# VectorE turns o of the first four blocks in phase 2, in 32 by 32 squares out of PSUM

## The chip, the cores and the metric

The kernel runs on one core of a Trainium2 chip. The metric is the device time in microseconds (us) of one execution; the median of three runs of the kernel before is 740.78 us (740.58 to 740.94).

## What is computed

`adj` is a 4096 x 4096 matrix, `x` is 4096 x 128, all in fp32. Two graph layers follow each other, each with a residual sum and a layer norm:

```python
scale = sum(d_list * filt * d_list, axis=0)
o = adj @ (scale[:, None] * (adj @ (x @ W0)))          # layer 0: z = adj @ x, v = scale * (z @ W0), o = adj @ v
x1 = layernorm(x + o + bias)
inn = (adj   / rowsum(adj))   @ x1 @ W_in              # layer 1: y
outt = (adj.T / rowsum(adj.T)) @ x1 @ W_out            # layer 1: z2
result = layernorm(x1 + inn + outt)
```

## The kernel before

`adj` is cut into 8 x 8 chunks of 512 x 512 (1 MB each). A chunk is loaded by SyncE into one of six ring slots (`raw`), ScalarE rounds it to `hi` (four activations of 128 x 512 where row sums are taken as well), and VectorE computes `lo = raw - hi` (`low(n)`, one instruction over 128 x 2048 in the phases of interest). A product of a chunk with a block of x or v is then 12 matmuls on TensorE (`product`): four of hi by the vector's high part, four of hi by its low part, four of lo by its high part (lines 647, 652, 657). The slot is free for the next load when TensorE has released the chunk. Each engine's instructions stand in an order written out by hand, all of it by the chunk number n; engines meet at counting semaphores only.

The result of a product lies in PSUM as features x rows (128 x 512 per block of 512 rows). The row-wise work needs rows x features, so the accumulator has to be turned.

Phase 1 (chunks below N1) computes z, v and the first part of o. Phase 2 (N1 to N2, 38 chunks) finishes o, block by block from I = 7 down to 0, and takes the first part of y from the same chunks: a chunk (J, I) with J > I is used for o and, behind it, for y (`y_product`). Blocks 7 to 4 have 7 - I chunks in phase 2, since their other part of o was saved in phase 1; blocks 3 to 0 (I < LEAD = 4) have 8 chunks each. The phase after N2 reads the other copy of adj for z2 and then the rest of y; it needs every x1 block in the order 7 to 0.

When o of block I is complete in `accB[:, I % 2]`, the following happens in phase 2, the numbers being chunk numbers after the block's last one, `last2[I]`:

- VectorE, after `low(last2 + 2)`: `o_sum(I)`. For blocks 3 to 0 this is one copy of 128 x 512 from PSUM to `turned` in SBUF (line 501).
- TensorE, after the products of `last2 + 2`: `turn_o(I)`, four transposes by the identity matrix of 128 x 128 each, from `turned` to the PSUM buffer `nat` (line 687). For block 0 this stands before the very last y product of the phase.
- VectorE, after `low(last2 + 4)`: `x1_block(I)` adds `nat` to the rows in SBUF (line 526) and takes the moments (lines 508, 511); ScalarE takes the square root in its turn (line 366) and can round no further chunk before it; then `x1_parts(I)` scales the rows and splits them into x_hi and x_lo (lines 535 to 539).

Only after that come `low(last2 + 5)` and the next ones. The chunk numbers of block 0 run over into the next phase: its `o_sum` stands behind `low(N2 + 1)`, its `x1_block` behind `low(N2 + 3)`.

Of the kernel before, what the change touches and what calls it, by code (L numbers as in the profile page):

```python
# [8 lines left out]
ALU = mybir.AluOpType  # L9
# [3 lines left out]
P = 128  # L13
TPB = 4
# [5 lines left out]
LEAD = 4  # L20


def graph_kernel(nc, x_t, adj_b, adjT_b, coef_t, W0, bias, W_in, W_out, ident_d, out):
# [10 lines left out]
    NB = adj_b.shape[0]  # L34
# [39 lines left out]
    w_out_at = {last_z2[J] + (3 + J - HB if J >= HB else 2): J for J in range(NB)}  # L74
    w_in_at = {last4[I] + 3: I for I in range(NB - 1)}
    assert not set(w_out_at) & set(w_in_at)
    NAT_H, NAT_Y = {}, {}
    for k, n in enumerate(sorted(list(w_out_at) + list(w_in_at))):
        if n in w_out_at:
            NAT_H[w_out_at[n]] = 2 * NB + k  # L80
        else:
            NAT_Y[w_in_at[n]] = 2 * NB + k
    NAT_Y[NB - 1] = 4 * NB - 1


    both = [n for n in range(N1, N2) if chunks[n][0] > chunks[n][1]]
    y_behind, y_rest = {}, list(both)
    for n in range(N1 + 3, N2):
        y_behind[n] = [m for m in y_rest if m <= n - (2 if n >= N1 + 6 else 3)]
        y_rest = y_rest[len(y_behind[n]):]  # L90
# [47 lines left out]
    def with_sums(n):  # L138

        J, I = chunks[n]  # L140
        return J <= I and I >= LEAD if n < N1 else n < N2 or is_z2[n]
# [4 lines left out]
    for n in range(N4):  # L146
        hi_at.append([hi_count + (t if n < LEAD * NB or with_sums(n) else 0) + 1 for t in range(TPB)])
        lo_at.append([lo_count + t * parts[n] // TPB + 1 for t in range(TPB)])
        hi_count, lo_count = hi_at[n][-1], lo_at[n][-1]


    NAT_O = NB

    def o_saved(I):

        return 2 * NB - 1 - LEAD - I

    with ExitStack() as ctx:
        def sb(name, shape, dt=F32):
            return ctx.enter_context(nc.sbuf_tensor(name, shape, dt))  # L160

        def pb(name, banks):
            return ctx.enter_context(nc.psum_tensor(name, [P, banks, BLK], F32))

        def sem(name):
            return ctx.enter_context(nc.semaphore(name))
# [16 lines left out]
        rows = sb("rows", [P, NT, P])  # L183
        part = sb("part", [P, NB - 1, BLK])
        turned = sb("turned", [P, 2, BLK])
# [21 lines left out]
        accB = pb("accB", 2)  # L207
        nat = pb("nat", 2)
# [28 lines left out]
        s_os = sem("o_taken")  # L237
        s_ty = sem("turned_y_ready")
        s_nat = sem("nat_read")
        s_x1 = sem("x1_ready")  # L240
# [7 lines left out]
        s_o = sem("o_done")  # L248
        s_n = sem("nat_filled")
# [9 lines left out]
        def block_of(I):  # L259
            return slice(TPB * I, TPB * I + TPB)  # L260
# [52 lines left out]
        def _(act):  # L313
# [38 lines left out]

            def turn_h(J):
                act.wait_ge(s_rel, rank[last_z2[J]])
                act.wait_ge(s_n, NAT_H[J] - 1)
                nc.scalar.activation(turned[:, NAT_H[J] % 2], z2_acc[J % HB], ACT.Copy).then_inc(s_tz, 1)

# [79 lines left out]
        def _(dve):  # L437
# [53 lines left out]

            def o_sum(I):
                u = 2 * NB - 1 - I
                dve.wait_ge(s_n, u - 1)
                if I == NB - 1:
                    dve.wait_ge(s_v, NB)
                    dve.wait_ge(s_rel, rank[N1 - 1])
                else:
                    dve.wait_ge(s_o, NB - 1 - I)
                if I < LEAD or I == NB - 1:  # L500
                    nc.vector.tensor_copy(turned[:, u % 2], accB[:, I % 2]).then_inc(s_os, 1)
                    return
                dve.wait_ge(s_os, o_saved(I) - 1)
                nc.vector.tensor_tensor(turned[:, u % 2], accB[:, I % 2], part[:, I], ALU.add).then_inc(s_os, 1)

            def moments(k, I, tiles):
                for t in tiles:
                    last = nc.vector.bn_stats(stats[:, t], rows[:, TPB * I + t])
                then(last)
                for t in tiles:  # L510
                    last = nc.vector.bn_aggr(mv[:, k % 2, t], stats[:, t])
                last.then_inc(s_var, 1)
# [9 lines left out]

            def x1_block(I):
                k = NB - 1 - I
                dve.wait_ge(s_n, NAT_O + k + 1)
                nc.vector.tensor_tensor(rows[:, block_of(I)], nat[:, k % 2].rearrange("p (t f) -> p t f", t=TPB),
                                        rows[:, block_of(I)], ALU.add).then_inc(s_nat, 1)
                dve.wait_ge(s_nat, k + 1)
                moments(k, I, range(TPB))

            def x1_parts(I):
# [23 lines left out]
            def update(r, t, bank):  # L555

                row = TPB * r + t
                return nc.vector.scalar_tensor_tensor(rows[:, row], bank[:, P * t:P * t + P], deg[:, 1, row:row + 1],  # L558
                                                      rows[:, row], ALU.mult, ALU.add)
# [63 lines left out]
            k = NB + r  # L623
            dve.wait_ge(s_out, k - NB - 1)
            for t in range(TPB):
                dve.wait_ge(s_n, NAT_Y[r] + t + 1)
                last = update(r, t, last_bank[t])
# [3 lines left out]
            for t in range(TPB):  # L631
                row = TPB * r + t
                last = nc.vector.tensor_scalar(rows[:, row], rows[:, row], mv[:, k % 2, t, 0:1],
                                               rstd[:, k % 2, t:t + 1], ALU.subtract, ALU.mult)
# [4 lines left out]
        def _(pe):  # L639
            def product(acc, r_hi, r_lo, K, n, first, last):  # L640

                h, l = hi[slot_of[n]], lo[slot_of[n]]

                def by_hi(t):
                    if t == 0 or hi_at[n][t] > hi_at[n][t - 1]:
                        pe.wait_ge(s_hi, hi_at[n][t])
                    nc.tensor.matmul(acc, r_hi[:, TPB * K + t], h[:, t], start=(first and t == 0), stop=False)  # L647
                    if n == 0 and t == 0:
                        pe.wait_ge(s_x0, 2)
                    elif n in x_from and t == 0:  # L650
                        pe.wait_ge(s_xlo, K)
                    nc.tensor.matmul(acc, r_lo[:, TPB * K + t], h[:, t], start=False, stop=False)  # L652

                def by_lo(t):
                    if t == 0 or lo_at[n][t] > lo_at[n][t - 1]:
                        pe.wait_ge(s_lo, lo_at[n][t])
                    return nc.tensor.matmul(acc, r_hi[:, TPB * K + t], l[:, t], start=False,  # L657
                                            stop=(last and t == TPB - 1))

                early = n == 0  # L660
                for t in range(TPB):
                    by_hi(t)
                    if early and t:
                        by_lo(t - 1)
                for t in range(TPB - 1 if early else 0, TPB):
                    mm = by_lo(t)
                return mm
# [15 lines left out]
            def transposes(e):  # L683
                room(e)
                for t in range(TPB):
                    to = slice(P * t, P * t + P)
                    mm = nc.tensor.transpose(nat[:, e % 2, to], turned[:, e % 2, to], ident[:])  # L687
                mm.then_inc(s_n, 1)
# [7 lines left out]
            def turn_o(I):  # L696
                pe.wait_ge(s_os, o_saved(I))
                if I == NB - 1:
                    pe.wait_ge(s_small, 16 * len(small))
                transposes(NAT_O + NB - 1 - I)  # L700
# [14 lines left out]
            def y_product(n):  # L715
                J, I = chunks[n]
                pe.wait_ge(s_x1, NB - J)
                if J == NB - 1:
                    pe.wait_ge(s_tz, NB)
                    if I <= NB - 4:  # L720
                        pe.wait_ge(s_ys, NB - 3 - I)
                product(accA[:, I % 2], x_hi, x_lo, J, n, J == NB - 1, J == I + 1).then_inc(s_rel, 1)
# [5 lines left out]
            for n in range(N1):  # L728
                J, I = chunks[n]
# [25 lines left out]
            for n in range(N1, N2):  # L755
                J, I = chunks[n]
                if n == first2[I]:
                    pe.wait_ge(s_os, o_saved(I + 2))
                mm = o_product(n, n == first2[I], n == last2[I])
                if n == last2[I]:  # L760
                    mm.then_inc(s_o, 1)
                elif J <= I:
                    mm.then_inc(s_rel, 1)
                if n == N1:
                    turn_o(NB - 1)
                for m in y_behind.get(n, []):
                    y_product(m)
                if n == N1 + 3:
                    turn_o(NB - 2)
                for I in range(NB - 3, 0, -1):  # L770
                    if n == last2[I] + (3 if I == NB - 3 else 2):
                        turn_o(I)
            for m in y_rest[:-1]:
                y_product(m)
            turn_o(0)
            y_product(y_rest[-1])

            for n in range(N2, N4):
                if is_z2[n]:
                    I, J = chunks[n]  # L780
# [7 lines left out]
                else:  # L788
                    J, I = chunks[n]
# [5 lines left out]
                if n in w_out_at:  # L795
                    J = w_out_at[n]
                    pe.wait_ge(s_tz, NB + J + 1)
                    by_rows(NAT_H[J], w_out)
                if n in w_in_at:
                    I = w_in_at[n]  # L800
# [3 lines left out]
            for t in range(TPB):  # L804
                to = slice(P * t, P * t + P)
# [34 lines left out]
```

## Time and profile before

| | value |
|---|---|
| median of three runs | 740.78 us |
| the profiled execution | 740.59 us |
| its span, first to last instruction | 738.8 us |
| TensorE busy | 728.8 us, 99% |
| VectorE busy | 564.1 us, 76% |
| ScalarE busy | 511.2 us, 69% |
| mean granted TensorE clock | 0.998 |

The profiled execution's own time is 1.8 us above its span. Times in the rows count from the start of the span. Phase 2 lies at about 261 to 442 us. A group in the rows is named by the line of the kernel; a row of the timeline gives the start, the length, and in brackets how long the engine had been idle and who ended that. Where a row says x4, the length is that of the four together, which overlap.

### The profile page before, as it was taken

What the parts mean: (1) busy time and instruction counts of PE and PEld (TensorE: products, weight loads), DVE (VectorE), ACT (ScalarE), POOL (GpSimd) and SP (SyncE); (2) the same over time, 40 slices, a digit from 0 to 9 for tenths busy, and PEclk for the clock granted to TensorE, in tenths of its full rate; (3) what the DMA queues carried; (4) which work ended last, traced back from release to release, by engine and by line L of the source; (5) the groups of instructions that cost most, each with busy time, mean ns of one, the idle gap of its engine ahead of it and who ended that gap; (6) DMA issues with size and microseconds to landing.
All of it is one profiled execution on the core that took longest, in us unless ns stands there. A gap on an engine that the chain in (4) does not pass through costs nothing.

```text
span 738.8 us, 9134 instructions
## 1 busy us (share of the span) xinstructions
PE 728.8 (99%) x3312; PEld 602.9 (82%) x3312; DVE 564.1 (76%) x663; ACT 511.2 (69%) x1304; POOL 18.5 (3%) x15
## 2 busy tenths in 40 slices
PE   8999999999999999999999999999999999999996
PEld 5888888888888888888888888888888888888885
DVE  5998987563735478867583748997898999999996
ACT  5888985734625454657474547998999888876862
POOL 1122200000000000000000000000000000000000
PEclk9999999999999999999999999999999999999999
DMA  8999995555545346776657459999999999999991
GB/s 345 424 426 421 427 412 185 200 215 212 201 160 199 138 159 241 265 273 244 228 171 254 151 217 374 386 385 386 365 335 389 385 365 383 383 354 351 348 360 34
DMA packets 35532, 217.02 MB, mean 294 GB/s; under 512 B 3616, under 2 KB 8480, under 8 KB 9760
## 3 DMA queue, kind: packets, MB, share of 16 engines
q1 hardware_dynamic: 35072, 215.79, 76.4%
q10 hardware_dynamic: 416, 0.66, 0.3%
q8 instruction: 26, 0.43, 0.2%
q14 instruction: 18, 0.15, 0.1%
HBM read 214.34 MB, written 2.10 MB: 293 GB/s over the span
## 4 chain that ended last, share of the span: by engine, by line
PE 96%; DMA 2%; DVE 1%; SPq 0%; ACT 0%; issue 0%; DVEq 0%
PE accA L647 14%; PE accA L652 14%; PE accA L657 14%; PE accB L647 12%; PE accB L652 12%; PE accB L657 12%; PE accC L657 6%; PE accC L647 6%; PE accC L652 6%; PE nat L680 3%; DMA raw<-in_adjT_b 2%; PE nat L687 0%; DVE lo L451 0%; SPq L280 0%; DVE rows L558 0%; ACT hi L329 0%
## 5 line engine op out<-in xcount | busy, mean ns | idle before, releaser
L451 DVE TENSOR_TENSOR lo<-raw,hi 128x2048 fp32r<-128x2048 f32 (+2 forms) x236 | 463.7, 1988 | 114.7 <-ACT hi L323 101.7
L323 ACT ACTIVATE hi<-raw 128x512 fp32r<-128x512 f32 x512 | 315.5, 622 | 70.2 <-DMA raw<-in_adjT_b 44.6
L647 PE MATMUL accA<-hi,x_hi 128*128 128x512 f32 x448 | 175.7, 392 | 1.9 <-ACT hi L329 1.9
L652 PE MATMUL accA<-hi,x_lo 128*128 128x512 f32 x448 | 174.4, 389 | 0.0
L657 PE MATMUL accA<-lo,x_hi 128*128 128x512 f32 x448 | 120.4, 389 | 0.1
L647 PE MATMUL accB<-hi,v_hi 128*128 128x512 f32 x256 | 100.4, 392 | 0.0
L647 PEld LDWEIGHTS accA<-hi,x_hi 128*128 128x128 f32 x448 | 84.2, 188 | 19.7 <-issue 2.4
L652 PE MATMUL accB<-hi,v_lo 128*128 128x512 f32 x256 | 99.7, 389 | 0.0
L657 PEld LDWEIGHTS accA<-lo,x_hi 128*128 128x128 f32 x448 | 84.0, 188 | 18.0 <-DVE lo L451 0.6
L652 PEld LDWEIGHTS accA<-hi,x_lo 128*128 128x128 f32 x448 | 84.1, 188 | 16.8
L323 ACT ACTIVATION_READ_ACCUMULATOR hi<-raw 128x1 f32 x512 | 97.3, 190 | 0.0
L331 ACT ACTIVATE hi<-raw 128x2048 fp32r<-128x2048 f32 x42 | 80.1, 1914 | 24.7 <-DMA raw<-in_adjT_b 24.7
L329 ACT ACTIVATE hi<-raw 128x512 fp32r<-128x512 f32 x128 | 70.3, 621 | 15.2 <-DMA raw<-in_adjT_b 15.1
L647 PE MATMUL accC<-hi,x_hi 128*128 128x512 f32 x192 | 75.0, 390 | 0.0
L652 PE MATMUL accC<-hi,x_lo 128*128 128x512 f32 x192 | 74.7, 389 | 0.0
L657 PE MATMUL accB<-lo,v_hi 128*128 128x512 f32 x256 | 68.5, 389 | 0.0
L657 PEld LDWEIGHTS accB<-lo,v_hi 128*128 128x128 f32 x256 | 48.1, 188 | 10.1
L647 PEld LDWEIGHTS accB<-hi,v_hi 128*128 128x128 f32 x256 | 48.1, 188 | 9.8
L652 PEld LDWEIGHTS accB<-hi,v_lo 128*128 128x128 f32 x256 | 48.1, 188 | 9.8
L657 PE MATMUL accC<-lo,x_hi 128*128 128x512 f32 x192 | 51.6, 390 | 0.1
L647 PE MATMUL accB<-hi,x_hi 128*128 128x512 f32 x128 | 50.3, 393 | 0.0
L652 PE MATMUL accB<-hi,x_lo 128*128 128x512 f32 x128 | 49.8, 389 | 0.0
(74 smaller groups left out, 454.7 us busy)
## 6 DMA issues: line engine op xcount, KB each, us to landing
raw<-in_adjT_b SPq DMA_DIRECT2D x137, 1024.0 KB, 4.9
raw<-in_adj_b SPq DMA_DIRECT2D x64, 1024.0 KB, 5.2
rows<-in_x_t SPq DMA_DIRECT2D x8, 256.0 KB, 10.7
out<-rows SPq DMA_DIRECT2D x7, 256.0 KB, 5.8
raw<-in_adjT_b ACTq DMA_DIRECT2D x1, 512.0 KB, 5.4
raw<-in_adjT_b SPq DMA_DIRECT2D x1, 512.0 KB, 6.7
out<-rows SPq DMA_DIRECT2D x1, 128.0 KB, 1.8
out<-rows ACTq DMA_DIRECT2D x1, 128.0 KB, 1.8
```

Of the source, the lines that this page charges most:

```text
L323: nc.scalar.activation(hi[slot][:, t], raw[slot][:, t], ACT.Copy, accum_out=to[:, TPB * K + t, C:C + 1]).then_inc(s_hi, 1)
L329: nc.scalar.activation(hi[slot][:, t], raw[slot][:, t], ACT.Copy).then_inc(s_hi, 1)
L331: nc.scalar.activation(hi[slot][:], raw[slot][:], ACT.Copy).then_inc(s_hi, 1)
L451: nc.vector.tensor_tensor(lo[slot][:, at], raw[slot][:, at], hi[slot][:, at], ALU.subtract).then_inc(s_lo, 1)
L647: nc.tensor.matmul(acc, r_hi[:, TPB * K + t], h[:, t], start=(first and t == 0), stop=False)
L652: nc.tensor.matmul(acc, r_lo[:, TPB * K + t], h[:, t], start=False, stop=False)
L657: return nc.tensor.matmul(acc, r_hi[:, TPB * K + t], l[:, t], start=False, stop=(last and t == TPB - 1))
L680: mm = nc.tensor.matmul(nat[:, e % 2, to], turned[:, e % 2, to], w[:], start=True, stop=True)
```

## The change

For blocks 3 to 0, `o_sum` no longer copies: VectorE reads `accB` in squares of 32 partitions by 32 columns and writes each square transposed to its place in `turned`. One instruction takes the four tiles of a block at once (32 x 4 x 32), so there are 16 instructions per block, in the place where the copy stood. `x1_block` of these blocks adds `turned` instead of `nat` and waits for nothing of TensorE. TensorE's `turn_o` of blocks 3 to 0 goes, and the numbers of the uses of `nat` behind it move down by four. ScalarE's first two copies to `turned` in the next phase get a wait for the last x1 block in addition, since VectorE now reads `turned` there.

```diff
             def o_sum(I):
                 u = 2 * NB - 1 - I
-                dve.wait_ge(s_n, u - 1)
+                if I >= LEAD - 2:
+                    dve.wait_ge(s_n, u - 1)
                 if I == NB - 1:
                     dve.wait_ge(s_v, NB)
                     dve.wait_ge(s_rel, rank[N1 - 1])
-                else:
-                    dve.wait_ge(s_o, NB - 1 - I)
-                if I < LEAD or I == NB - 1:
                     nc.vector.tensor_copy(turned[:, u % 2], accB[:, I % 2]).then_inc(s_os, 1)
+                    return
+                dve.wait_ge(s_o, NB - 1 - I)
+                if I < LEAD:
+                    of = accB[:, I % 2].rearrange("p (t n) -> p t n", t=TPB)
+                    to = turned[:, u % 2].rearrange("p (t f) -> p t f", t=TPB)
+                    for a in range(0, P, 32):
+                        for b in range(0, P, 32):
+                            last = nc.vector.transpose(to[b:b + 32, :, a:a + 32], of[a:a + 32, :, b:b + 32])
+                    last.then_inc(s_os, 1)
                     return
...
             def x1_block(I):
                 k = NB - 1 - I
-                dve.wait_ge(s_n, NAT_O + k + 1)
-                nc.vector.tensor_tensor(rows[:, block_of(I)], nat[:, k % 2].rearrange("p (t f) -> p t f", t=TPB),
-                                        rows[:, block_of(I)], ALU.add).then_inc(s_nat, 1)
-                dve.wait_ge(s_nat, k + 1)
+                if I < LEAD:
+                    dve.wait_ge(s_os, o_saved(I))
+                    then(nc.vector.tensor_tensor(rows[:, block_of(I)], rows[:, block_of(I)],
+                                                 turned[:, (NB + k) % 2].rearrange("p (t f) -> p t f", t=TPB), ALU.add))
...
             def turn_h(J):
                 act.wait_ge(s_rel, rank[last_z2[J]])
+                if NAT_H[J] < 2 * NB - LEAD + 2:
+                    act.wait_ge(s_x1, NB)
...
-                for I in range(NB - 3, 0, -1):
+                for I in range(NB - 3, LEAD - 1, -1):
                     if n == last2[I] + (3 if I == NB - 3 else 2):
                         turn_o(I)
-            for m in y_rest[:-1]:
+            for m in y_rest:
                 y_product(m)
-            turn_o(0)
-            y_product(y_rest[-1])
```

On TensorE the end of phase 2 read before as follows; `accA<-lo5` is the last but one y product, `accA<-hi2` the last, and `nat<-ident` the turn of block 0:

```order
1643 L652 MATMUL accA<-hi5_66,x_lo 128x512
1644 L657 MATMUL accA<-lo5_65,x_hi 128x512 [waits lo_ready]
1645 L657 MATMUL accA<-lo5_65,x_hi 128x512 x3
1646 L687 MATMUL nat<-ident,turned 128x128 [waits nat_read,o_taken]
1647 L687 MATMUL nat<-ident,turned 128x128 x3
1648 L647 MATMUL accA<-hi2_57,x_hi 128x512 [waits hi_ready,x1_ready]
```

The same place with the change:

```order
1637 L668 MATMUL accA<-hi5_66,x_lo 128x512
1638 L673 MATMUL accA<-lo5_65,x_hi 128x512 [waits lo_ready]
1639 L673 MATMUL accA<-lo5_65,x_hi 128x512 x3
1640 L663 MATMUL accA<-hi2_57,x_hi 128x512 [waits hi_ready,x1_ready]
1641 L668 MATMUL accA<-hi2_57,x_lo 128x512
```

The four transposes are gone, and nothing stands in their place. Likewise at the turns of blocks 3, 2 and 1.

On VectorE, block 0 at the start of the next phase, before; `lo3`, `lo0`, `lo1` are the subtractions of chunks N2 + 1, N2 + 2 and N2 + 3:

```order
247 L451 TENSOR_TENSOR lo3_59<-raw3_58,hi3_60 128x2048 [waits hi_ready,dve_step]
248 L501 COPY turned<-accB 128x512 [waits o_done,nat_filled]
249 L451 TENSOR_TENSOR lo0_50<-raw0_49,hi0_51 128x2048 [waits hi_ready]
250 L451 TENSOR_TENSOR lo1_53<-raw1_52,hi1_54 128x2048 [waits hi_ready]
251 L526 TENSOR_TENSOR rows<-nat,rows 128x512 [waits nat_filled]
252 L508 BN_STATS stats<-rows 128x6 [waits nat_read]
```

And with the change:

```order
250 L454 TENSOR_TENSOR lo3_59<-raw3_58,hi3_60 128x2048 [waits hi_ready,dve_step]
251 L511 STREAM_TRANSPOSE turned<-accB 32x4x32 [waits o_done]
252 L511 STREAM_TRANSPOSE turned<-accB 32x4x32 x15
253 L454 TENSOR_TENSOR lo0_50<-raw0_49,hi0_51 128x2048 [waits hi_ready]
254 L454 TENSOR_TENSOR lo1_53<-raw1_52,hi1_54 128x2048 [waits hi_ready]
255 L538 TENSOR_TENSOR rows<-rows,turned 128x512 [waits o_taken]
256 L519 BN_STATS stats<-rows 128x6 [waits dve_step]
```

Sixteen instructions stand where one did, ahead of two subtractions for which TensorE will ask, and the sum that follows them no longer waits for TensorE.

## Rows read from the trace of the kernel before

**Rows 1.** Page, parts 1 and 2: busy time by engine, and TensorE's clock in 40 slices

```profile
PE 728.8 (99%) x3312; PEld 602.9 (82%) x3312; DVE 564.1 (76%) x663; ACT 511.2 (69%) x1304; POOL 18.5 (3%) x15
...
PEclk9999999999999999999999999999999999999999
```

**Rows 2.** Waits of TensorE over the whole span: total, times, longest

```profile
PE accA L647 <- ACT hi L329: 1.9, 1, 1.9
PE accB L726 <- DVE warm L577: 1.2, 1, 1.2
PE accB L807 <- ACT turned L412: 0.4, 1, 0.4
```

**Rows 3.** The chain that ended last, around blocks 3, 2, 1, 0: start, length, what

```profile
333.59 0.91 PE accA L657 x4
334.50 0.44 PE nat L687 x4
336.79 0.92 PE accB L657 x4
...
369.44 0.91 PE accA L657 x4
372.63 0.91 PE accB L657 x4
...
405.27 0.91 PE accB L657 x4
407.99 0.91 PE accA L657 x4
...
411.19 0.92 PE accB L657 x4
...
441.13 0.91 PE accA L657 x4
...
444.32 0.91 PE accA L657 x4
```

**Rows 4.** Groups by line on VectorE: shapes, count, busy, mean ns of one

```profile
L508 DVE BATCH_NORM_STATS2 stats<-rows 128x6 f32<-128x128 f32 x64 | 14.0, 281 | 0.5
L558 DVE SCALAR_TENSOR_TENSOR rows<-nat,deg,rows 128x128 f32<-128x128 f32 x28 | 7.8, 342 | 0.0
L501 DVE COPY turned<-accB 128x512 f32<-128x512 f32 x5 | 3.4, 688 | 2.5 <-PE accB L657 2.5
```

**Rows 5.** Timeline of VectorE around block 0: start, length, instruction, idle before

```profile
438.15 0.69 DVE L501 COPY turned<-accB 128x512 f32<-128x512 f32 x1
443.68 2.29 DVE L451 TENSOR_TENSOR lo<-raw,hi 128x2048 fp32r<-128x2048 f32 x1 [4.84 <-ACT hi L323]
446.67 2.29 DVE L451 TENSOR_TENSOR lo<-raw,hi 128x2048 fp32r<-128x2048 f32 x1 [0.70 <-ACT hi L323]
448.88 0.69 DVE L526 TENSOR_TENSOR rows<-nat,rows 128x512 f32<-128x512 f32 x1
...
454.29 4.65 DVE L451 TENSOR_TENSOR lo<-raw,hi 128x2048 fp32r<-128x2048 f32 x2
```

**Rows 6.** Timeline of TensorE's weight loads for the lo matmuls of chunk N2 + 4

```profile
457.53 0.87 PEld L657 LDWEIGHTS accC<-lo,x_hi 128*128 128x128 f32 x4
```

**Rows 7.** Timeline of VectorE around block 3

```profile
323.72 0.69 DVE L501 COPY turned<-accB 128x512 f32<-128x512 f32 x1 [1.30 <-PE accB L657]
...
334.97 0.69 DVE L526 TENSOR_TENSOR rows<-nat,rows 128x512 f32<-128x512 f32 x1 [4.27 <-PE nat L687]
...
340.38 4.65 DVE L451 TENSOR_TENSOR lo<-raw,hi 128x2048 fp32r<-128x2048 f32 x2
```

**Rows 8.** Timeline of VectorE around blocks 2 and 1

```profile
356.85 0.69 DVE L501 COPY turned<-accB 128x512 f32<-128x512 f32 x1 [1.20 <-PE accB L657]
...
366.83 2.29 DVE L451 TENSOR_TENSOR lo<-raw,hi 128x2048 fp32r<-128x2048 f32 x1 [5.43 <-ACT hi L323]
...
396.76 0.68 DVE L501 COPY turned<-accB 128x512 f32<-128x512 f32 x1
...
405.34 2.29 DVE L451 TENSOR_TENSOR lo<-raw,hi 128x2048 fp32r<-128x2048 f32 x1 [3.06 <-ACT hi L323]
409.38 0.69 DVE L526 TENSOR_TENSOR rows<-nat,rows 128x512 f32<-128x512 f32 x1 [1.74 <-PE nat L687]
```

**Rows 9.** Stretch of 442.5 to 520 us: busy by engine, clock, DMA share

```profile
442.50:520.00 77.50, 77.50 (x343) 64.14 (x343) 65.81 (x46) 68.14 (x219) 0.00 (x0) 1.00 0.98 383
```

More of the change, by code:

```diff
@@ L79, in graph_kernel @@
         if n in w_out_at:
-            NAT_H[w_out_at[n]] = 2 * NB + k
+            NAT_H[w_out_at[n]] = 2 * NB - LEAD + k
         else:
-            NAT_Y[w_in_at[n]] = 2 * NB + k
-    NAT_Y[NB - 1] = 4 * NB - 1
+            NAT_Y[w_in_at[n]] = 2 * NB - LEAD + k
+    NAT_Y[NB - 1] = 4 * NB - LEAD - 1
     both = [n for n in range(N1, N2) if chunks[n][0] > chunks[n][1]]
@@ L524, in x1_block @@
                 k = NB - 1 - I
-                dve.wait_ge(s_n, NAT_O + k + 1)
-                nc.vector.tensor_tensor(rows[:, block_of(I)], nat[:, k % 2].rearrange("p (t f) -> p t f", t=TPB),
-                                        rows[:, block_of(I)], ALU.add).then_inc(s_nat, 1)
-                dve.wait_ge(s_nat, k + 1)
+                if I < LEAD:
+                    dve.wait_ge(s_os, o_saved(I))
+                    then(nc.vector.tensor_tensor(rows[:, block_of(I)], rows[:, block_of(I)],
+                                                 turned[:, (NB + k) % 2].rearrange("p (t f) -> p t f", t=TPB), ALU.add))
+                else:
+                    dve.wait_ge(s_n, NAT_O + k + 1)
+                    nc.vector.tensor_tensor(rows[:, block_of(I)], nat[:, k % 2].rearrange("p (t f) -> p t f", t=TPB),
+                                            rows[:, block_of(I)], ALU.add).then_inc(s_nat, 1)
+                    dve.wait_ge(s_nat, k + 1)
                 moments(k, I, range(TPB))
```

## The prediction

> **What bounds the kernel now.** Read the page's engine shares first: TensorE is busy 728.8 us of a span of 738.8, at the full granted clock in every slice (2.4 GHz, of the two levels) [rows 1]. Then its waits: in the whole span it waited three times, 3.5 us together, and none of the three is in phase 2 or the phase behind it (they are the first product, the warm-up and the last four matmuls) [rows 2]. So from the second product to the last one TensorE runs without a hole, and the chain that ended last is TensorE's own row of matmuls [rows 3]. Two things follow. Whatever leaves TensorE's queue shortens the kernel by the time it took there; and whatever happens on VectorE costs nothing until a subtraction (`lo`) is finished later than TensorE asks for it. VectorE has 24% of idle time as a mean, but the mean doesn't decide; what does is the slack at the four places where work is added.
>
> **TensorE: four turns go.** I read their price from the pace of the products. Without a turn the lo matmuls of two successive products start 2.72 us apart (405.27 to 407.99). With a turn between them the distance is 3.20 (333.59 to 336.79), 3.19 (369.44 to 372.63), 3.20 (407.99 to 411.19) and 3.19 (441.13 to 444.32) [rows 3]. The excess is 0.48 + 0.47 + 0.48 + 0.47 = 1.90 us. The transposes themselves are only 0.44 of each in the chain; the few hundredths left are slightly wider steps of the first matmuls behind them, which go too. No wait is in that excess (TensorE had none), so all of it comes back: -1.90 us. The wait for `o_taken` that stood before each turn goes at no gain.
>
> **VectorE: 16 transposes for one copy, four times.** The trace shows no such instruction. Call T the time of the 16. Each handles 128 elements per partition out of PSUM. Lower bound: the nearest small instructions in a row, each starting before the last has ended. The mean step is 14.0 us / 64 = 0.22 for the statistics over 128 elements (SBUF) and 7.8 / 28 = 0.28 for the PSUM operand; T is 3.5 to 4.5 us. If instead each starts when the last has ended, the durations count: 16 x 0.342 = 5.5 us. Upper bound: each takes as long as the copy of the whole bank, 16 x 0.688 = 11.0 us, as if the square cost four times the pace of a copy [rows 4]. Between ends this far apart I take 5.5, from the row that is nearest (a PSUM operand, 128 elements, full duration), because successive transposes write other partitions than the one before and I see no row in which that overlaps.
>
> The Trainium skill bears on just that: "VectorE: DVE Perf Modes", section "Two Vector instructions with no wait between them", says that an instruction whose output starts in another group of 32 partitions than the last output waits until all earlier ones have finished. By it all 16 are held, and T is the 5.5 rather than the 4.5; no run here has shown it yet.
>
> **What hides T.** Block 0 is the tight place. The copy starts at 438.15; the next subtraction starts at 443.68 because ScalarE isn't done with its chunk before [rows 5]. So T may be 443.68 - 438.15 = 5.53 us and nothing moves at all. There are 0.70 us of idle time before the next subtraction (446.67), so up to 6.23 the sum at 448.88 starts where it did. From there VectorE runs through the moments and the parts and reaches the subtraction of N2 + 4 at 454.29; one takes 2.29, so it ends at 456.58 [rows 5]. TensorE loads the weights of its lo matmuls at 457.53 [rows 6]: slack 0.95. With block 0's turn gone TensorE comes 0.47 earlier against VectorE (the three earlier turns shift both alike, since VectorE's place here is set by ScalarE, the loads and TensorE's releases), which leaves 0.48. Hence TensorE waits if T is above 6.23 + 0.48 = 6.71 us, that is 0.42 us per transpose. With T = 5.5 it waits for nothing.
>
> Block 3: the transposes start at 323.72. The two subtractions behind them need 4.65 and may then start when VectorE pleases; before, the sum waited until 334.97 for TensorE's turn, 4.27 us of it idle [rows 7]. Now it needs T + 4.65 from 323.72, so up to T = 334.97 - 323.72 - 4.65 = 6.6 the sum is not later than it was. The subtraction behind x1_parts starts at 340.38 and ends at 342.67 [rows 7]; it is that of last2 + 5, whose lo matmuls stand three products behind the one at 336.79 (last2 + 3, last2 + 4, a y product, last2 + 5), at 336.79 + 3 x 2.72 = 344.95. Their weights are loaded 0.4 us ahead, and the turn's 0.48 goes: 344.95 - 0.4 - 0.48 = 344.07, a slack of 1.4. So block 3 bears T up to 6.6 + 1.4 = 8.0. Blocks 2 and 1: from the copy to the second subtraction behind it are 366.83 - 356.85 = 9.98 and 405.34 - 396.76 = 8.58 us, of which the first subtraction needs 2.29; so T is free up to 7.7 and 6.3 us, and the idle 1.74 us that the sum of block 1 waited for the turn is more reserve [rows 8]. None of these is as tight as block 0.
>
> **The rest, at nothing.** The sum in `x1_block` reads SBUF rather than PSUM at the same 128 x 512 elements; it is one instruction behind cover in each block. ScalarE's first new wait stands behind its chunk N2 + 31, some 26 chunks of 2.72 us behind the x1 block for which it waits, so it costs nothing. The renumbering of `nat` moves no instruction. Loads are asked for by TensorE's releases; in the stretch behind phase 2 the DMA engines are at 0.98 and 383 GB/s [rows 9], but that is TensorE's own pace (1.05 MB per 2.72 us is 386 GB/s), and since every load is asked for 1.90 us earlier, it lands earlier as well.
>
> The sum against the profiled execution: 740.59 - 1.90 = 738.69 us, span 738.8 - 1.9 = 736.9. The profiled execution lies 0.19 below the median of the runs shown, so the median should be 740.78 - 1.90 = 738.88 us, 0.26% less. What a measurement of this kernel can tell from no change is about 0.2%, or 1.48 us.
>
> **Rival A, a part is given back at block 0.** T lies between 7.1 and 9: then TensorE waits at chunk N2 + 4 for T - 6.71 (and at block 3 for T - 8.0 above that). At T = 8 the time is 740.78 - 1.90 + 1.3 = 740.2; at T = 9 with both waits, it is 740.78 - 1.90 + 2.3 + 1.0 = 742.2. All of this case is "no difference". For it: fp32 squares of 32 at half the pace of a copy would add 0.13 us each to 0.342, T = 7.6. Against it: every other VectorE instruction in the rows runs fp32 out of PSUM at the pace of its elements (512 in 0.688 us, 128 in 0.342) [rows 4].
>
> **Rival B, slower.** The place is the same, the lo of N2 + 4, and block 3 joins. The price: at T = 11.0 TensorE waits 11.0 - 6.71 = 4.3 us behind block 0 and 11.0 - 8.0 = 3.0 behind block 3, 740.78 - 1.90 + 7.3 = 746.2. The kernel gets slower from T of about 9.05 (0.57 us per transpose) on, where the two waits together exceed 1.90 + 1.48. Against it: it wants a transpose that costs nearly as much as a whole bank's copy, on a quarter of the elements. In the skill, "VectorE: DVE Perf Modes", section "The three transpose paths", has VectorE at 311 ns for 128 x 128 in bf16, in squares of 32; by that figure, an estimate, T would be about 5.0. The same page's rules send a 128 x 128 transpose to TensorE; the rows say the reverse is paid for here, because the time is taken from the engine that has no idle time and given to one that has.
>
> **Rival C, the turns give nothing.** If the excess of 0.48 around a turn were a wait of TensorE's queue that another wait would replace, such as the next chunk's `hi`, the time would stay 740.8. The waits of TensorE speak against it: none is listed there [rows 2].
>
> **How the numbers follow.** Forecast (T below 6.7, or a wait of less than 0.42): 0.77, of which a little is lost to the bound lying only 0.4 us from the gain. Rival A 0.13, rival B 0.06, rival C 0.04. So faster by over 0.2% is 0.75; within 0.2% 0.18; slower 0.07. The likeliest time is 738.9. The range takes the forecast with the scatter of the runs (0.2 us either side), and rival A's lower half: 738.4 to 740.2.
>
> **What would show it.** Products at 2.72 us across all four former turns; 16 transposes at 0.34 us or less per step; no wait of TensorE for `lo` between 440 and 470 us; the sum of block 3 earlier than 334.97, and that of block 1 about 1.7 us earlier; the next subtraction of block 0 still waiting for ScalarE, if briefly. Wrong would be: a step above 0.42 us, and with it a wait of TensorE for the `lo` of N2 + 4 about 16 us behind the end of block 0's o.

## The result, and the profile after

Twelve runs of the kernel after have a median of 739.02 us (738.70 to 739.28), twelve of the kernel before 740.82 us. The ratio is 0.9974 with a 95% interval of 0.9966 to 0.9981: 1.80 us less, where 1.90 were forecast. The profiled execution took 738.70 us with a span of 736.9 us; before it was 740.59 and 738.8, so 1.89 less in one and 1.9 in the other.

The page of the kernel after, parts 1 and 2, answers to [rows 1]:

```profile
PE 727.3 (99%) x3296; PEld 601.5 (82%) x3296; DVE 581.2 (79%) x723; ACT 511.7 (69%) x1304; POOL 18.6 (3%) x15
...
PEclk9999999999999999999999999999999999999998
```

TensorE has 16 instructions fewer, VectorE is busy 17.1 us longer, and the time still fell. The waits of TensorE after are the same three as in [rows 2], with nothing in phase 2:

```profile
PE accA L663 <- ACT hi L330: 1.7, 1, 1.7
PE accB L742 <- DVE warm L593: 1.2, 1, 1.2
PE accB L821 <- ACT turned L415: 0.4, 1, 0.4
```

The chain that ended last, after, at the places of the four former turns (start, length, what), answers to [rows 3]:

```profile
333.60 0.91 PE accA L673 x4
336.32 0.91 PE accB L673 x4
...
368.96 0.91 PE accA L673 x4
371.68 0.91 PE accB L673 x4
...
407.04 0.91 PE accA L673 x4
409.76 0.91 PE accB L673 x4
...
439.68 0.91 PE accA L673 x4
442.40 0.91 PE accA L673 x4
```

All four distances are 2.72 us now. The first pair starts where it did (333.60 against 333.59); the lo matmuls of the last product of phase 2 start at 442.40 against 444.32, 1.92 us earlier. From there to the end of the span it is 294.5 us in both, so nothing is added or lost behind it.

VectorE after: all transposes, and its timeline around block 3, which answers to [rows 7]:

```profile
L511 DVE STREAM_TRANSPOSE turned<-accB x64: 303/312/323, 323.7 to 441.7; 32x128 f32<-32x128 f32 x64
```

```profile
323.73 5.20 DVE L511 STREAM_TRANSPOSE turned<-accB 32x128 f32<-32x128 f32 x16 [1.31 <-PE accB L673]
328.97 4.49 DVE L454 TENSOR_TENSOR lo<-raw,hi 128x2048 fp32r<-128x2048 f32 x2
333.38 0.69 DVE L538 TENSOR_TENSOR rows<-rows,turned 128x512 f32<-128x512 f32 x1
...
338.77 4.65 DVE L454 TENSOR_TENSOR lo<-raw,hi 128x2048 fp32r<-128x2048 f32 x2
```

T, the time of the 16, is 5.20 us: one transpose takes 0.312 us, and the next starts 0.325 after it. The two subtractions follow without a pause, and the sum starts at 333.38, which is 1.6 us earlier than before, although VectorE had 4.5 us more to do: before, it had stood still 4.27 us for TensorE's turn and 1.7 us for ScalarE.

Block 0 after, which answers to [rows 5], and the weight loads that answer to [rows 6]:

```profile
436.79 5.21 DVE L511 STREAM_TRANSPOSE turned<-accB 32x128 f32<-32x128 f32 x16
442.03 2.29 DVE L454 TENSOR_TENSOR lo<-raw,hi 128x2048 fp32r<-128x2048 f32 x1
445.36 2.29 DVE L454 TENSOR_TENSOR lo<-raw,hi 128x2048 fp32r<-128x2048 f32 x1 [1.04 <-ACT hi L324]
447.57 0.68 DVE L538 TENSOR_TENSOR rows<-rows,turned 128x512 f32<-128x512 f32 x1
...
452.96 4.66 DVE L454 TENSOR_TENSOR lo<-raw,hi 128x2048 fp32r<-128x2048 f32 x2
```

```profile
455.61 0.87 PEld L673 LDWEIGHTS accC<-lo,x_hi 128*128 128x128 f32 x4
```

The lo of N2 + 4 is the first of the two subtractions in the row at 452.96. It ends at 452.96 + 2.29 = 455.25 and is wanted at 455.61. The reserve was 0.95 us and is 0.36; 0.48 was forecast. Of T, 1.04 us more fit before the sum moves, and 0.36 more before TensorE waits: the bound is 6.6 us (forecast 6.71).

### The profile page after: what moved, and what is told of

The parts are those of the page before. It is cut to its first block, busy times and chain, and to the rows that moved or that the text cites. A ratio compares the mean times of both kernels' runs of the same rounds, so it can differ in the third digit from the quotient of the medians.

```text
span 736.9 us, 9156 instructions
## 1 busy us (share of the span) xinstructions
PE 727.3 (99%) x3296; PEld 601.5 (82%) x3296; DVE 581.2 (79%) x723; ACT 511.7 (69%) x1304; POOL 18.6 (3%) x15
## 4 chain that ended last, share of the span: by engine, by line
PE 96%; DMA 2%; DVE 1%; SPq 0%; ACT 0%; issue 0%; DVEq 0%
PE accA L663 14%; PE accA L668 14%; PE accA L673 14%; PE accB L663 12%; PE accB L668 12%; PE accB L673 12%; PE accC L673 6%; PE accC L668 6%; PE accC L663 6%; PE nat L696 3%; DMA raw<-in_adjT_b 2%; DVE lo L454 0%; PE nat L703 0%; SPq L281 0%; DVE rows L574 0%; ACT hi L330 0%
```

## Experiments

**1. The four turns put back as dead work.**

```diff
+            def dead_turn(I):
+                pe.wait_ge(s_nat, NB - LEAD)
+                for t in range(TPB):
+                    to = slice(P * t, P * t + P)
+                    nc.tensor.transpose(nat[:, (NB - 1 - I) % 2, to], ident[:], ident[:])
...
+                for I in range(LEAD - 1, 0, -1):
+                    if n == last2[I] + 2:
+                        dead_turn(I)
-            for m in y_rest:
+            for m in y_rest[:-1]:
                 y_product(m)
+            dead_turn(0)
+            y_product(y_rest[-1])
```

> The kernel after, with TensorE's four turns of blocks 3 to 0 put back in their old places as dead work: four transposes of the identity matrix each into the free buffer nat, which nobody reads and nobody waits for. VectorE still does the real turning. Theory Q (what the change gained is the time of the four turns in TensorE's queue, and VectorE's part is free): 739.0 + 1.9 = 740.9 us, and the distance between lo matmuls across a turn is 3.20 again. Rival W (the gain is in the waits: x1_block no longer waits for TensorE, so ScalarE and VectorE run ahead): stays at 739.0 to 739.3.

Measured: 741.04 us, ratio to before 1.0001 (0.9992 to 1.0010); the kernel before took 740.98 us on the same chip. The chain shows the old distance again, 337.16 - 333.96 = 3.20:

```profile
333.96 0.91 PE accA L673 x4
334.87 0.44 PE nat L722 x4
337.16 0.92 PE accB L673 x4
```

Here x1_block waits for no turn, VectorE and ScalarE have the work and the order of the kernel after, and the whole gain is gone. So it is TensorE's time, and the removed waits of the others were worth nothing that can be measured. Theory Q stands, W falls.

**2. A copy instead of the 16 transposes.**

```diff
-                    for a in range(0, P, 32):
-                        for b in range(0, P, 32):
-                            last = nc.vector.transpose(to[b:b + 32, :, a:a + 32], of[a:a + 32, :, b:b + 32])
+                    last = nc.vector.tensor_copy(to, of)
```

> The kernel after, with one copy of 128 x 512 in place of the 16 transposes (so o of blocks 3 to 0 is added unturned; the result is not the reference's there). VectorE has 4 x 4.5 = 18 us less to do. Theory Q: the transposes are hidden entirely, so 739.0 (738.9 to 739.1). Rival: VectorE's added work costs something by its load on SBUF and PSUM or by small delays: 738.5 or less.

Measured: 739.09 us, ratio 0.9974 (0.9965 to 0.9984), as the kernel after. The eighteen microseconds (4 x 4.5) by which the transposes take longer than a copy cost nothing. Its timeline around block 0 also shows how much room there is without them:

```profile
437.05 0.68 DVE L509 COPY turned<-accB 128x512 f32<-128x512 f32 x1
440.14 2.29 DVE L454 TENSOR_TENSOR lo<-raw,hi 128x2048 fp32r<-128x2048 f32 x1 [2.41 <-ACT hi L324]
445.61 2.29 DVE L454 TENSOR_TENSOR lo<-raw,hi 128x2048 fp32r<-128x2048 f32 x1 [3.17 <-ACT hi L324]
```

The first subtraction starts 440.14 - 437.05 = 3.1 us behind the copy, not 5.53 as in [rows 5]. There ScalarE's rounding of that chunk started 2.9 us behind the start of the copy, since it waited for the load; in all thirteen other traces it starts 0.3 to 0.7 us behind the start of the copy or of the transposes. Only one trace of the kernel before is kept, so it is not shown whether the late load belongs to that execution or to that kernel. The second stands 8.56 us behind the copy's start (8.52 in [rows 5]), and less 2.29 for the first that is a bound of 6.3 us for T, as forecast.

**3. Sixteen more transposes at block 0.**

```diff
+                    squares = [(a, b) for a in range(0, P, 32) for b in range(0, P, 32)]
+                    spare = part[:, I].rearrange("p (t f) -> p t f", t=TPB)
+                    for a, b in squares[:16] if I == 0 else []:
+                        nc.vector.transpose(spare[b:b + 32, :, a:a + 32], of[a:a + 32, :, b:b + 32])
...
```

> The kernel after, with 16 more transposes of accB ahead of block 0's own, into a part of SBUF that nobody reads before it is overwritten. T of block 0 goes from 5.2 to 10.4 us. Theory S (what VectorE may take is the slack at chunk N2 + 4, up to T = 6.25 without a shift and 6.61 without a wait, from the trace after; forecast 6.71): TensorE waits 10.4 - 6.6 = 3.8 us once for the lo of N2 + 4: 742.8 us. Rival M (VectorE is busy 79% on the mean, so 5.2 us more are absorbed): 739.0.

Measured: 742.90, 744.35, 742.76 and 744.40 us, ratio 1.0035 (1.0021 to 1.0049). The profiled one is of 742.90. Its waits of TensorE, those that are new:

```profile
PE accC L676 <- DVE lo L454: 2.2, 1, 2.2
...
PE accC L666 <- ACT hi L324: 0.7, 1, 0.7
```

It is chunk N2 + 4, as forecast; ScalarE is late as well there, since its square root waits for VectorE's moments (454.21 us) and the rounding of N2 + 4 stands behind it. The chain in this trace:

```profile
457.65 2.21 DVE lo L454
459.86 0.04 issue
459.91 1.20 PE accC L676 x4
462.93 0.91 PE accC L676 x4
```

Against the kernel after, the next lo matmuls (those of N2 + 5) start 462.93 - 458.72 = 4.2 us later. This execution's TensorE was 0.41 us behind already before the wait (by the timelines its lo matmuls of N2 + 3 start at 453.53 against 453.12). That leaves 3.8 for a forecast of 3.8; the two executions of 742.8 us lie 3.8 us above the median of the kernel after as well.

The two waits make 2.9 us of the 3.8. The rest is in wider steps. The hi matmuls of the chunk follow ScalarE's activations of 0.61 us each (pairs start at 455.26, 455.80, 456.39 and 457.01, where 0.45 apart is usual), and the first matmuls behind the long wait are slower too. The timeline of TensorE has there:

```profile
459.91 1.20 PE L676 MATMUL accC<-lo,x_hi 128*128 128x512 f32 x4 [2.16 <-DVE lo L454]
...
462.76 1.07 PE L676 MATMUL accC<-lo,x_hi 128*128 128x512 f32 x4
```

That is 2.85 us from lo matmuls to lo matmuls, where 2.72 is usual. M falls: a mean idle share of VectorE of 21% absorbs nothing beyond the 6.6 us at this place. The second group of times is taken up in experiment 9.

**4. Sixteen more at block 3 instead** (the same edit with `I == 3`).

> The same 16 more transposes at block 3 instead of block 0, T = 10.4 us there. Theory S with that block's own slack (forecast bound 8.0; from the trace after the lo of last2 + 5 ends at 341.06 and its weights are loaded at 344.1, so 5.2 + 3.0 = 8.2): TensorE waits 2.2 us for that lo: 741.2 us. If the bound of a block were the same everywhere, 742.8 as at block 0; by rival M 739.0.

Measured: 741.23 us, ratio 1.0003 (0.9994 to 1.0013): 2.2 us more than the kernel after, as theory S had it, from the block's own reserve (10.4 - 2.2 = 8.2). The wait is again for the lo behind x1_parts:

```profile
PE accB L676 <- DVE lo L454: 1.6, 2, 1.4
```

**5. Eight more at block 0** (the edit against experiment 3).

```diff
-                    for a, b in squares[:16] if I == 0 else []:
+                    for a, b in squares[:8] if I == 0 else []:
```

> The kernel after with 8 more transposes at block 0 (half of the earlier padding), T = 24 x 0.325 = 7.8 us. Theory S: TensorE waits for all of what T has above 6.6 us and for nothing below it: 7.8 - 6.6 = 1.2 us, 739.0 + 1.2 = 740.2 us, with one wait, for the lo of N2 + 4. If instead the price were proportional to the added work (16 more cost 3.8 to 4.6 us), 8 more would cost 1.9 to 2.3 us: 740.9 to 741.3.

Measured: 739.76 us, ratio 0.9987 (0.9978 to 0.9996), so 0.7 us above the median of the kernel after, which was not measured beside it. On the same chip as this run the kernel of experiment 6, whose block 0 is that of the kernel after, took 738.64 us, which makes it 1.1. The profiled chain has the lo matmuls of N2 + 5 at 459.74 against 458.72, 1.0 us later. All three are nearer to 1.2 than to 1.9 or more. Together with experiment 3 the price is a line with a threshold, not a proportion: T of 5.2, 7.8 and 10.4 costs 0, 1.0 and 3.8 us in the traces. From 7.8 to 10.4 the price rises by 2.8 for 2.6 us of T, about one for one.

**6. The squares in another order.**

```diff
+                    squares = [(a, b) for a in range(0, P, 32) for b in range(0, P, 32)]
+                    if I == 3:
+                        squares = [(a, b) for b in range(0, P, 32) for a in range(0, P, 32)]
+                    if I == 1:
+                        squares = [(a, (a + k) % P) for k in range(0, P, 32) for a in range(0, P, 32)]
+                    tiles = [slice(0, 2), slice(2, 4)] if I == 2 else [slice(0, 4)]
+                    for a, b in squares:
+                        for t in tiles:
+                            last = nc.vector.transpose(to[b:b + 32, t, a:a + 32], of[a:a + 32, t, b:b + 32])
```

> The kernel after with the squares in another order: block 3 with the column of squares outside (the output stays in one group of 32 partitions for four instructions, the input changes), block 1 along diagonals (both change each time), block 2 with each square cut in two instructions of two tiles, the same input and output partitions twice; block 0 as it was. Theory H (an instruction starts only when the last has ended if either its input or its output starts in another group of 32 partitions than before): blocks 3 and 1 keep T = 5.2 us; in block 2 the second of each pair (0.245 us long) starts before the first has ended, as the statistics do (a step some 0.08 shorter than the duration), so T = 16 x (0.26 + 0.16) = 6.7 us. Rival (transposes never overlap): block 2 takes 32 x 0.26 = 8.3 us. Rival (the output alone decides): block 3 takes 12 x 0.24 + 4 x 0.325 = 4.2 us. The time stays at 739.0 in all cases but the 8.3 us, which would cost some tenths.

Measured: 738.64 us, ratio 0.9973 (0.9962 to 0.9984). Blocks 3, 2 and 1 in its timeline:

```profile
323.70 5.21 DVE L517 STREAM_TRANSPOSE turned<-accB 32x128 f32<-32x128 f32 x16 [1.34 <-PE accB L679]
...
356.34 6.33 DVE L517 STREAM_TRANSPOSE turned<-accB 32x64 f32<-32x64 f32 x32 [1.27 <-PE accB L679]
...
395.81 5.21 DVE L517 STREAM_TRANSPOSE turned<-accB 32x128 f32<-32x128 f32 x16
```

Three orders, one T of 5.21: it is enough that either side changes its partitions. In block 2 three single instructions, one behind the other, are:

```profile
356.51 0.20 DVE L517 STREAM_TRANSPOSE turned<-accB 32x64 f32<-32x64 f32 x1
356.72 0.24 DVE L517 STREAM_TRANSPOSE turned<-accB 32x64 f32<-32x64 f32 x1
356.90 0.20 DVE L517 STREAM_TRANSPOSE turned<-accB 32x64 f32<-32x64 f32 x1
```

From the first of a pair (356.72, 0.24 long) to the second, on the same partitions, it is 0.18, so they overlap. From the second of the pair before (356.51, 0.20 long) to the next pair it is 0.21: that one waits for the end. Theory H holds, and both rivals fall: 6.33 us for block 2 is far from 8.3, and 5.21 for block 3 from 4.2. The 0.4 us by which 6.33 is under the forecast of 6.7 come from the steps: the held one is 0.21 where 0.26 was taken, the overlapping one 0.18 where it was 0.16.

**7. VectorE turns block 4 too, in the old place** (the limits of the change go from 4 to 5 blocks, with this sum ahead of the transposes).

```diff
-                if I < LEAD:
+                if I < TURN:
+                    if I >= LEAD:
+                        dve.wait_ge(s_os, o_saved(I) - 1)
+                        then(nc.vector.tensor_tensor(accB[:, I % 2], accB[:, I % 2], part[:, I], ALU.add))
```

> VectorE turns block 4 too (sum with the saved part in place in PSUM, then 16 transposes), in the old place behind low(last2 + 2); TensorE's turn of block 4 goes. TensorE's queue gives back 0.48 us. But VectorE has no idle time there: it goes from x1 of block 5 straight on. In the trace after, its sum of block 4 starts at 295.4; with 5.9 us of sum and transposes the lo of last2 + 3 ends at 303.6 and is wanted at 302.8, and x1_block comes 4 us later, so the lo of last2 + 5 ends at 313.5 and is wanted at 311.8. Theory S: -0.48 + 1.7 = +1.2, 740.2 us. Rival Q alone (each turn taken off TensorE gains its 0.48): 738.5.

Measured: 740.70 us, ratio 1.0000 (0.9991 to 1.0009). The turn taken away is more than given back. The loss is 1.7 us against the median of the kernel after, not measured beside it, and 2.1 us against the kernel of experiment 6 (738.64) on the same chip. In the traces it is 1.95: the lo matmuls of the last product of phase 2 start at 444.50 against 442.40 in the chains, and 0.15 of that this execution was behind already ahead of block 4. The direction was right, the size of 1.2 was 0.8 too small, by a slip in my sum: the two late subtractions cost 0.8 and then, on top of it, 1.7; I had counted only the second, and 2.5 - 0.48 is 2.0. TensorE's wait in the trace, and VectorE's timeline there:

```profile
PE accB L676 <- DVE lo L455: 1.8, 2, 1.3
```

```profile
295.54 0.69 DVE L509 TENSOR_TENSOR accB<-accB,part 128x512 f32<-128x512 f32 x1
296.27 5.20 DVE L514 STREAM_TRANSPOSE turned<-accB 32x128 f32<-32x128 f32 x16
301.50 4.49 DVE L455 TENSOR_TENSOR lo<-raw,hi 128x2048 fp32r<-128x2048 f32 x2
...
311.31 4.66 DVE L455 TENSOR_TENSOR lo<-raw,hi 128x2048 fp32r<-128x2048 f32 x2
```

**8. The same, at a place with room.**

```diff
-                    if n == last2[I] + (3 if I == NB - 3 else 2):
+                    if n == last2[I] + (3 if I == NB - 3 else 4 if I == 4 else 2):
                         o_sum(I)
-                    if n == last2[I] + 4:
+                    if n == last2[I] + (6 if I == 4 else 4):
                         x1_block(I)
```

(and ScalarE's square root for it moves by two chunks as well)

> As the one before it, but block 4's sum and transposes stand behind low(last2 + 4), and its x1_block, x1_parts and ScalarE's square root behind chunk last2 + 6, where the lo are ahead of TensorE. Theory S: every lo is in time (tightest last2 + 7, 0.9 us of slack), so the whole 0.48 us comes: 738.5 us. If block 4's x1 or the lo are late by more than I work out, 739 to 740.

Measured: 738.47 us, ratio 0.9968 (0.9956 to 0.9981). TensorE waits nowhere in phase 2. In the timeline of TensorE the lo matmuls on either side of the former turn of block 4 start at 300.42 and 303.14, 2.72 us apart; in the kernel after they start at 300.32 and 303.52, 3.20 apart. Between different chips 0.5 us isn't told apart, so this kernel and the kernel after ran again on one chip:

> The kernel after once more, on the same chip and beside the next one. 738.9 to 739.0; its distance to the next one is what is asked.

> The kernel in which VectorE turns block 4 too, behind low(last2 + 4), once more. Theory Q: 0.48 us less than the kernel after on this chip, with spans that differ by the same once the times of the first product are taken off. If it is level with it, the fifth turn is paid for elsewhere.

Measured: 739.02 us (ratio 0.9975, 0.9965 to 0.9985) and 738.54 us (ratio 0.9970, 0.9958 to 0.9981). The difference of the medians is 0.48 us, the price of one turn. The intervals of the two ratios overlap, but five of the six executions (738.36 to 738.55) lie below all nine of the kernel after (738.72 to 739.23); the sixth, at 739.44, is the profiled one, and experiment 9 says where it lost its time. So theory Q holds for the fifth turn too, by the gap in the timelines and by these executions together. This version is the fastest measured. With experiment 7 it shows that the same 5.9 us of VectorE's work cost 2.0 us net or gain 0.5, by where they stand.

**9. The two groups of times.** The kernel of experiment 3 twice more.

> The kernel with 16 more transposes at block 0 once more, for its trace: its runs fell into two groups, about 742.8 us (two) and 744.4 us (two). Theory S gives 742.8 and has no second group. Theory C: TensorE's idle time of some 3 us at chunk N2 + 4 lets its granted clock fall for a while in some executions; then a trace at 744.4 shows slices behind 460 us at a lower clock or products above 2.72 us apart. Theory L: a load or ScalarE comes late as well, then there is a second wait.

> The same kernel a third time, for the same question: 742.8 us with products 2.72 us apart behind the wait, or 744.4 us with a place that shows where 1.6 us more go (theory C: a lower granted clock; theory L: a second wait).

Measured: 744.28 and 742.67 us, one of each group. The stretches of 455 to 460 and 460 to 465 us (busy by engine, granted clock, DMA), in the execution of 744.28:

```profile
455.00:460.00 5.00, 2.83 (x9) 1.51 (x10) 4.87 (x8) 5.00 (x17) 0.00 (x0) 0.96 0.68 274
460.00:465.00 5.00, 5.00 (x17) 3.91 (x16) 4.68 (x3) 5.00 (x19) 0.00 (x0) 0.70 0.45 152
```

and in the one of 742.67:

```profile
455.00:460.00 5.00, 2.81 (x9) 1.49 (x10) 4.82 (x9) 5.00 (x16) 0.00 (x0) 1.00 0.67 277
460.00:465.00 5.00, 5.00 (x23) 4.13 (x22) 4.67 (x3) 5.00 (x18) 0.00 (x0) 1.00 0.59 210
```

The waits of TensorE before it are the same 2.2 us for lo in both. In one the granted clock then is 0.70 as a mean of five microseconds, that is 1.2 GHz for a good part of them, and TensorE gets through 17 matmuls instead of 23. Its timeline has single matmuls start 0.43 us apart there (461.37, 461.79, 462.22), where 0.23 is usual, until 463.04. In its chain it is from the lo matmuls after the wait to the next ones 464.14 - 459.52 = 4.62 us instead of 3.02:

```profile
459.52 2.05 PE accC L676 x4
464.14 0.92 PE accC L676 x4
466.88 0.91 PE accB L676 x4
```

1.6 us, the distance of the two groups. Theory C holds; L falls, since there is no wait in one that isn't in the other. The low clock is seen in this one trace. The other two executions of the slower group (744.35 and 744.40 us) have no trace; their mean clock of 0.996 and 0.994, against 0.998 in all three of the faster group, says the same of them. Why the clock fell in three of six executions with the same waits is open.

It is not only the added work that brings it. The profiled execution of 739.44 us in experiment 8 waited 2.2 us for the hi of its first product, and its stretches of 5 to 10 and 10 to 15 us read:

```profile
5.00:10.00 5.00, 2.79 (x10) 1.45 (x9) 2.05 (x4) 1.60 (x4) 0.00 (x0) 0.90 1.02 404
10.00:15.00 5.00, 5.00 (x18) 3.95 (x18) 4.38 (x6) 4.43 (x10) 0.00 (x0) 0.76 1.02 424
```

The clock is 0.90 and 0.76, and the execution is 0.9 us above the median of its kernel. In the trace of experiment 3 the same wait was 2.4 us, and the clock stayed at 1.00. Single executions of other kernels that lie 0.6 to 1.0 us above their median have a mean clock of 0.995 or 0.996 too, one of the kernel before among them (741.79 us, 0.995); where they lost it isn't on record.

## Why the prediction was right

- **TensorE, -1.90 us.** Right: the excess of a turn between two products was 3.20 - 2.72, all of it came back (442.40 against 444.32, -1.92), and experiment 1 takes it away again by putting only the turns back. Rival C, that the excess hid a wait, has nothing left.
- **T.** Taken at 5.5 from the row of the nearest duration, 5.20 measured. The time doesn't test it: any T below 6.6 gives the same, and the copy of 0.7 us in experiment 2 did; it is the trace that does. The lower bound of 3.5 to 4.5, from instructions that overlap, was wrong because these don't: the trace after has steps of 0.325 with durations of 0.312. By what the Trainium skill states ("VectorE: DVE Perf Modes", section "Two Vector instructions with no wait between them") they shouldn't, and experiment 6 agrees: changing the partitions on the input side alone, on the output side alone or on both gives the same T, and a pair that keeps both overlaps.
- **The cover.** Right in size: the bound at block 0 was 6.71, the trace after gives 6.6, experiments 3 and 5 find the wait at the named chunk and its price at 3.8 and 1.0 us. One step on the way was wrong: I took the 5.5 us from the copy to the next subtraction as the rule. That was a late load in the one trace of the kernel before; experiment 2 has 3.1, and in the kernel after the subtraction followed the transposes without the pause that I had named as a sign. The sum still held because the reserve that decides lies one subtraction further. Block 3's bound of 8.0 is confirmed within 0.2 by experiment 4 (2.2 us for T = 10.4).
- **What hides where.** Block 3's sum came 1.6 us earlier. Block 1's started at 406.70 against 409.38 in [rows 8], 2.68 earlier, of which 0.95 is the gain of the two turns before it: 1.7, as forecast. Its row after is

```profile
406.70 0.69 DVE L538 TENSOR_TENSOR rows<-rows,turned 128x512 f32<-128x512 f32 x1
```

- **Rivals A and B** needed T above 7.1 and 9. Experiments 3, 4 and 5 made such T and got waits in their places, so the mechanism was real and only its size was missing. What I had not seen is that a wait of TensorE can cost more than its length. At a T near 9 the 1.6 us of the lower clock could come on top in some executions, and B would begin sooner; that T was not run. Rival A's 0.13 us for a square at half pace is not in the rows: the copy and the 0.342 us instruction give (0.688 - 0.342) / 3 = 0.115 for 128 elements, T = 7.3, which is still A.
- **The rest at nothing.** No wait of ScalarE's two new ones, the loads or the renumbering shows; the time from 442.40 to the end is the time from 444.32 before.

## What to carry to other kernels

Where one engine never waits, price what you take from it by the change in pace around it (here 0.48 us a turn), not by its busy time or length. Price what you give to the other engine by the deadline of the next thing that the first will ask for: in this kernel the work was free up to a threshold of 6.6 us at one block and 8.2 at another, then cost about one for one, and moving the same work by two chunks turned a loss of 2.0 us into a gain of 0.5. Before adding a wait to TensorE where it has none, count its clock as well: here the fall cost 1.6 us on top of 3.8 in three executions of six.

## What the runs showed of the hardware that was not expected

- A transpose of 32 x 4 x 32 fp32 from PSUM on VectorE takes 0.312 us and costs 0.325 in a row; one of half the size takes 0.20 to 0.24. There is no penalty for the square over the 0.342 of another instruction with 128 elements per partition.
- After a hole in TensorE's work with a single wait of 2.2 us for lo and one of 0.5 to 0.7 for hi, the granted clock fell in one of the three traced executions, and by their time and mean clock in three of six; the next product took 4.62 us instead of 3.02. With the shorter waits of experiments 4, 5 and 7 (the longest 1.4 us) the profiled executions show a mean clock of 0.997 to 0.998, as without. One of the ten executions of experiment 5 took 740.74 us with 0.996; it has no trace.
- The product behind a wait takes longer even at full clock: 2.85 us in the timeline from its lo matmuls to the next ones (459.91 to 462.76 in experiment 3, 456.73 to 459.58 in experiment 5) instead of 2.72. The chain has 3.02 for the same, but 0.17 of that is its way of counting: in a row without a wait it starts a group at the end of the matmul before (458.72 in the kernel after, where the timeline has 458.56). Where the 0.13 us come from is open.
- The deadline of a lo is the start of its weight load, as in [rows 6], not that of its matmul. In experiments 3 and 5 the lo ends 3.8 and 1.0 us behind the time at which the kernel after loads these weights (455.61, and 0.41 and 0.04 more for how far the two executions were behind), which is the price found; counted from the matmuls' start it would be 0.2 less.
